# A graph network layer on one core: part of one square moved from ScalarE to the Pool, and x split without its scale factor

## What is computed

```
# first layer: 4 gaussian kernels k over the entries of adj
w[k]  = exp(-0.5 * (adj - mean[k])**2 / (1e-14 + precision[k]**2))
w     = w / sum_k w
ws[k] = sum over the row of w[k]                     # one number per row and kernel
h     = concat_k(ws[k] * (x @ W0[k].T))
x     = layernorm(x + h)
# second layer: one expert per batch, chosen by the batch's mean of x
z     = adj @ x ;  o = z @ expert_w[top1]
y     = relu(batchnorm over all batches of one expert (o))
out   = layernorm(x + y)
```

## Time and profile before

| | |
|---|---|
| timed runs | median 892.62 us, 890.96 to 893.26 |
| the profiled execution | 888.44 us, its span 886.7 us |
| TensorE's mean granted clock | 0.952 |
| PE / DVE / ACT / POOL busy | 751.8 / 754.0 / 766.9 / 687.5 us |
| DMA | 191.71 MB, mean 216 GB/s |

### The profile page before, as it was taken

The page is one execution under the profiler, slowest core; times in us unless marked ns, Lnnn a source line. Parts: engine busy times, 40 slices in busy tenths (PEclk is TensorE's granted clock), DMA queues, the critical chain, the costliest instruction groups (busy, mean ns, idle before and its releaser), DMA issues.

```text
span 886.7 us, 12501 instructions
## 1 busy us (share of the span) xinstructions
PE 751.8 (85%) x3922; PEld 349.1 (39%) x3922; DVE 754.0 (85%) x1639; ACT 766.9 (86%) x774; POOL 687.5 (78%) x773
## 2 busy tenths in 40 slices
PE   1444469899999999999999999999999989996671
PEld 1111124344444444444444444444444434444440
DVE  1999988899999999999999999999999981226994
ACT  5999998999999999999999999999999941116983
POOL 6699999999988888888888888888888441004794
PEclk9966679999999999999999999999999999998996
DMA  8799886898897779777977797789786636219999
GB/s 229 200 282 257 189 243 166 221 202 206 201 240 192 192 190 240 196 194 190 237 198 191 195 240 196 192 189 242 198 190 161 124 141 263 95 64 396 356 383 366
DMA packets 263925, 191.71 MB, mean 216 GB/s; under 512 B 210098, under 2 KB 210098, under 8 KB 262322
## 3 DMA queue, kind: packets, MB, share of 16 engines
q1 hardware_dynamic: 263714, 190.90, 79.3%
q10 hardware_dynamic: 144, 0.00, 0.0%
HBM read 91.78 MB, written 48.76 MB: 159 GB/s over the span
## 4 chain that ended last, share of the span: by engine, by line
ACT 38%; DVE 27%; POOL 19%; PE 9%; issue 4%; DMA 1%; SPq 0%; POOLq 0%; DVEq 0%; ACTq 0%
DVE ps_t L953 19%; ACT wgt L647 13%; ACT ps_t L656 6%; ACT ps_t L658 6%; ACT adj_in L641 5%; ACT ps_t L652 5%; PE ps_z L1118 5%; POOL adj_cut L505 3%; DVE x_in L937 3%; DVE wgt L915 3%; PE ps_o L1136 2%; POOL adj_in L500 2%; POOL x_turn L516 2%; PE ps_t L1136 2%; POOL adj_cut L503 2%
## 5 line engine op out<-in xcount | busy, mean ns | idle before, releaser
L1118 PE MATMUL ps_z<-adjT,x1p 128*128 128x512 f16 x1536 | 341.7, 379 | 0.5 <-POOL x1p L542 0.5
L953 DVE TENSOR_TENSOR ps_t<-ps_t,wgt 128x1024 f32<-128x1024 f32 x192 | 234.8, 1223 | 28.0 <-ACT ps_t L652 26.9
L1104 PE MATMUL ps_h<-w0T,x_turn 128*128 128x512 f16 x768 | 194.5, 407 | 75.1 <-DVE x_in L937 64.2
L915 DVE SCALAR_TENSOR_TENSOR wgt<-wgt,ps_t 128x1024 f32<-128x1024 f32 x192 | 224.7, 1214 | 15.8 <-ACT ps_t L658 15.8
L1118 PEld LDWEIGHTS ps_z<-adjT,x1p 128*128 128x128 f16 x1536 | 150.0, 98 | 181.3 <-POOL x1p L542 1.0
L641 ACT ACTIVATE wgt<-adj_in,neg_mu 128x1024 f32<-128x1024 f32 x192 | 205.6, 1134 | 8.4 <-POOL adj_in L500 8.2
L647 ACT ACTIVATE wgt<-wgt 128x3072 f32<-128x3072 f32 x64 | 176.5, 2758 | 0.0
L1136 PE MATMUL ps_o<-zT,w_sel 128*128 128x512 f16 x696 | 159.7, 379 | 4.8 <-DVE zT L884 3.5
L1104 PEld LDWEIGHTS ps_h<-w0T,x_turn 128*128 128x128 f16 x768 | 75.0, 103 | 184.4 <-issue 105.1
L505 POOL TENSOR_TENSOR adj_cut<-adj_in,adj_cut 128x1024 f16<-128x1024 f32 x64 | 136.6, 2134 | 5.4
L1136 PEld LDWEIGHTS ps_o<-zT,w_sel 128*128 128x128 f16 x696 | 67.9, 98 | 87.7 <-DVE zT L884 4.5
(11 more groups left out here) (220 smaller groups left out, 774.2 us busy)
## 6 DMA issues: line engine op xcount, KB each, us to landing
adj_in<-in_adj_dram SPq DMA_DIRECT2D x64, 512.0 KB, 4.1
x_in<-in_x_dram SPq DMA_DIRECT2D x64, 256.0 KB, 4.3
x_spill<-x_in SPq DMA_DIRECT2D x28, 512.0 KB, 3.4
out_spill<-o_stage SPq DMA_DIRECT2D x50, 256.0 KB, 3.1
w_sel<-w_planes SPq DMA_DIRECT2D x8, 1024.0 KB, 7.5
adjT<-x_spill SPq DMA_DIRECT2D x6, 1024.0 KB, 10.1
out_dram<-adjT SPq DMA_DIRECT2D x5, 1024.0 KB, 6.7
adjT<-out_spill SPq DMA_DIRECT2D x4, 1024.0 KB, 12.7
```

The lines of the kernel that those rows point to most:

```text
L915: v.scalar_tensor_tensor(out=wgt[:, m % 2, j, :], in0=wgt[:, m % 2, j, :], scalar=SUM_SCALE / W0_SCALE, in1=tot, op0=ALU.mult, op1=ALU.mul ...
L953: v.tensor_tensor(tot, tot, wgt[:, n % 2, j, :], ALU.add).then_inc(dve_tot, 1)
L1104: last = te.matmul(ps_h[:, n % 2, :], xT[:, n % 2, left, c, :], w0T[:, right, c, :], start=(c + i == 0), stop=(c == C - 1 and i == 2))
L1118: last = te.matmul(ps_z[:, u % 2, :], x1p[:, b % 2, left, t, k * P:(k + 1) * P], adjT[:, b % 2, right, t, half * HALF:(half + 1) * HALF], ...
```

## The change

The Pool makes the fourth kernel's square for columns 0 to 255 of adj's tile, in place: a `tensor_scalar` with the spread and the shift of the kernel as per-partition scalars, and a `tensor_tensor` product of the result with itself. It does so in iteration n for tile n, behind cut_x(n+2) and ahead of norm_pair, after ScalarE's three other squares of that tile. ScalarE's fourth square covers the other 768 columns, and its fourth exp, which covers all 1024, waits for the Pool's product. The product of x by 16 on the Pool is gone: x is cut as it is, and the constant in L523 is adapted.

```diff
-X_SCALE = 2.0 ** 4
+POOL_SQ = 256
...
                 pool.wait_ge(x_landed[m % X_RING], 16 * (m // X_RING + 1))
-                g.tensor_scalar(tile, tile, X_SCALE, 1.0, ALU.mult, ALU.mult).then_inc(pool_xs, 1)
-                pool.wait_ge(pool_xs, m + 1)
                 wait(pool, x_turned[m % 2], 16 * (m // 2))
...
+            def square(m):
+
+                cols = adj_in[:, m % ADJ_RING, 0:POOL_SQ]
+                pool.wait_ge(act_sq, NK * m + NK - 1)
+                g.tensor_scalar(cols, cols, spread_of[:, SOLO:SOLO + 1], neg_mu[:, SOLO:SOLO + 1],
+                                ALU.mult, ALU.add).then_inc(pool_line, 1)
+                pool.wait_ge(pool_line, m + 1)
+                g.tensor_tensor(cols, cols, cols, ALU.mult).then_inc(pool_sq, 1)
...
-                g.tensor_scalar(rstd[:, p % 2, :], y_mv[:, p % 2, :, 1], X1_SCALE ** -2, LN_EPS * (X_SCALE / X1_SCALE) ** 2,
+                g.tensor_scalar(rstd[:, p % 2, :], y_mv[:, p % 2, :, 1], X1_SCALE ** -2, LN_EPS / X1_SCALE ** 2,
...
                     cut_x(n + 2)
+                if n < TILES:
+                    square(n)
...
-            def square(n, k, to):
-                s.activation(to, adj_in[:, n % ADJ_RING, :], ACT.Square, bias=neg_mu[:, k:k + 1],
+            def square(n, k, to, first=0):
+                s.activation(to, adj_in[:, n % ADJ_RING, first:NR], ACT.Square, bias=neg_mu[:, k:k + 1],
                              scale=spread[k]).then_inc(act_sq, 1)
...
                 act.wait_ge(act_sq, NK * n + NK)
+                act.wait_ge(pool_sq, n + 1)
...
-                    square(n, SOLO, adj_in[:, n % ADJ_RING, :])
+                    square(n, SOLO, adj_in[:, n % ADJ_RING, POOL_SQ:NR], POOL_SQ)
```

More of the change, by code:

```diff
@@ L162, in gnn_program @@
         pool_as, pool_ah, pool_al = (sem(f"pool_{k}") for k in ("as", "ah", "al"))
-        pool_xs, pool_xh, pool_xl = (sem(f"pool_{k}") for k in ("xs", "xh", "xl"))
+        pool_xh, pool_xl = (sem(f"pool_{k}") for k in ("xh", "xl"))
+        pool_line, pool_sq = sem("pool_line"), sem("pool_sq")
         pool_neg, pool_x1, pool_1h, pool_1l = (sem(f"pool_{k}") for k in ("neg", "x1", "1h", "1l"))
```

## The result

The changed kernel takes 901.92 us (median, 901.12 to 905.01), the kernel before 891.79 beside it: a ratio of 1.0133, 95% interval 1.0115 to 1.0151. So it is slower, as forecast, by 10 to 12 us and not by 27.8. The profiled execution took 902.38 us, its span 900.6, against 888.44 and 886.7 before.

A forecast was written before the change was run, and what follows sets the result against it. The four-exp loop through ScalarE and VectorE bounded, then the Pool would: P(60) = 47.3 + 29 x 22.38 + 5.3 = 701.6, tile 63's fourth exp +27.8 us. On 892.6 that gives 920.4 us, range 909 to 931.

The forecast's parts named there:

- The start: Tile 0's fourth exp waits for the Pool's product, moving from 17.76 to 25.2 us: +7.4 us, passed on to later tiles.
- Where the Pool's lateness bites: At even tiles the fourth exp can't start before P(n) + 7.85 us; P(n) is Pool iteration n's start.
- the net cost on the Pool: Per tile on the Pool: square added at 1.40 us, product of x removed at 0.70, net +0.70 us.
- The Pool becomes the bound: In the middle the Pool needs 22.38 us for two tiles, over the kernel's 21.91: 11.19 us a tile.
- ScalarE's loop would take 10.76: ScalarE's chain of exps and fourth square: 256 columns fewer save 0.20 us a tile, from 10.96.
- rival C: Square so cheap that ScalarE's loop bounds again: 12.4 us gained, 7.4 lost at the start; 887.6 us; chance 0.04.
- A: Pool's product of two f32 tensors goes by bytes, 0.84 us; two tiles 22.72 us, +10 us: 930; chance 0.14.
- B: Late start is taken up: P(2) stays at 39.86 us, adj tile 3 getting out another way; 913; chance 0.11.
- D: No change: a Pool square of 0.87 to 0.96 us, two effects cancel; 893 us; chance 0.04 together with between.
- The base: Profiled 888.4 + 27.8 gives 916.2 us; the timed median of 892.6, 4.2 above the profile, makes it 920.4.

The follow-up runs named there:

- Experiment 2: Changed kernel with tile 0 squared by ScalarE alone, its exp waiting for nothing of the Pool; 897.54 us, ratio 1.0066 to the kernel before.
- experiment 9: Changed kernel with 128 columns on the Pool, its product taken with a constant f32 tile instead of with itself; 901.10 us.
- experiment 3: Changed kernel without the Pool's square, ScalarE's whole again; only the product of x by 16 is removed; 891.19 us, ratio 1.0003 to the kernel before.
- experiment 5: Changed kernel with 512 columns of the square on the Pool; 940.86 us.
- experiment 4: Changed kernel with the Pool's product of x by 16 put back; 952.40 us.
- experiment 1: Changed kernel with the Pool's square only from tile 12 on, earlier tiles squared by ScalarE alone; 886.63 us, ratio 0.9959 to the kernel before.
- experiment 8: Changed kernel without the Pool's square, ScalarE squaring only 768 or 256 columns, the others left out; 884.22 and 883.89 us.
- experiment 6: Changed kernel with 128 columns instead of 256 on the Pool; 900.64 us, ratio 1.0122 to the kernel before.

## Why the prediction was wrong

The direction and the start were right, the middle was mis-sized. The direction came out right for part of the reason only: of the forecast 27.8 us, 7.4 belonged to the start and the rest was to build up over all tiles, but in the trace the lag is 17.4 us at tile 10 and shrinks from there. Step by step:

- *The start.* Forecast: fourth exp of tile 0 at 25.2, the Pool on tile 3 at 47.3. Measured: 24.63 and 46.97. Experiment 2 shows that the one hangs on the other.
- *Where the Pool's lateness bites.* Right in kind: at even tiles, by the product's end, 7.5 us into the Pool's iteration (7.85 forecast), and P(60) = P(2) + 29 pairs + the instructions slowed by VectorE. With the measured 21.84 this gives 46.97 + 633.4 + 5.5 = 685.9; the trace has 686.73.
- *The term that failed* is the net cost on the Pool, forecast +0.70 us a tile, measured (21.83 - 20.99) / 2 = +0.42. The product took 0.61 us instead of 0.67 (experiment 9: one tile read twice is cheaper than two). I gave each of the two new instructions a gap, and the first has none: 0.09. And with L511 another gap of 0.12 went away (experiment 3). Together 0.27; times 58 that is 15.7 us, most of the 18.5 us by which I missed (4.5 of these are the base, see the last point).
- *The Pool becomes the bound:* false, but narrowly. It is the bound up to tile 10; after that its 21.84 us are level with the loop's 21.81 to 21.90, and the lead of 0.6 to 1.0 us lasts to the end. With 0.64 and 0.81 us a tile more it bounds the whole middle (experiments 5 and 4), and at 21.89 us a pair the last 16 tiles (experiment 1).
- *ScalarE's loop would take 10.76.* False: 10.88, and in two tiles of each batch 11.01 and 10.95, for a reason that I had not looked for. The row sums end close ahead of the fourth exp even in the trace of before (the third L915 and the L652 after it):

```profile
405.19 1.22 DVE L915 SCALAR_TENSOR_TENSOR wgt<-wgt,ps_t 128x1024 f32<-128x1024 f32 x1
```

```profile
406.61 1.03 ACT L652 ACTIVATE ps_t<-adj_in 128x1024 f32<-128x1024 f32 x1
```

406.41 and 406.61, of which the hand-over takes 0.1: 0.1 us is all that ScalarE could gain. Here the error hardly counts for the time, since it enters three times at the end, but rival C's gain of 12.4 us never was there; with this part of the square free the medians give 6 to 7 and the trace 3.5 at tile 63 (experiment 8).
- *Rivals.* A went the wrong way for this kernel: one tile read twice is cheaper than the row. Two different f32 tiles are dearer than the row, 457 ns against 429 at 128 columns, though less than A's slope would make it (0.18 + 128 x 2.54 ns = 0.51 us). By the Trainium skill (GPSIMD Engine Reference, section 3.1) the read port takes two operands in turn; my estimate from its figure was 0.72 us for this product. The trace has 0.61 for one tile twice, so the measurement goes against the figure here. For two different tiles an estimate from experiment 9, with the fixed part of 186 ns kept and (457 - 186) / 128 = 2.12 ns a column, gives 0.73 for 256 columns, near the page's. B fell with experiment 2's start. C and D needed a square of at most 0.96 us with its gaps, 0.26 over the removal; it costs 0.42 over it.
- *The base.* The profiled execution of before lay 3.4 us under its median and that of after 0.5 over it, so the 13.9 us between the profiles are 10 to 12 between the runs. Adding a profile's difference to a median carries that error.

## What to carry to other kernels

Work that moves to an engine which runs ahead of its consumer costs nothing only where the lead exists: look at the lead at the start too, where it isn't built up yet, and begin the moved part when it is there (here: one condition, from 1.013 to 0.996). Before a step of a loop is shortened, look for what else ends just ahead of the same instruction: a second wait that is met 0.1 us early caps the gain at 0.1 us. When a change moves all later tiles in time, a one-time wait elsewhere can come or go with it (here 1.1 to 1.4 us ahead of tile 14); take it out before traces are compared. When two rates come out within a few per cent of each other, a gap of 0.08 us counts like a duration; take it from a pair of neighbours of the same kind, or keep both results.

## What the runs showed of the hardware

- A Pool product of one f32 tile with itself in place: 399, 612 and 1040 ns at 128, 256 and 512 columns, 1.67 ns a column, against 1.90 for f32 with f16, and 457 ns at 128 columns for two different f32 tiles (experiments 6, 5, 9 and the changed kernel).
- With the product of x by 16 gone, the Pool's faster pace let it meet VectorE's split of the expert weights (L977, two tiles in SBUF) in another place (x_only):

```profile
69.09 2.13 POOL L508 TENSOR_TENSOR adj_cut<-adj_in,adj_cut 128x1024 f16<-128x1024 f32 x1
69.21 3.09 DVE L977 SCALAR_TENSOR_TENSOR zT<-adjT,zT 128x1024 f16<-128x1024 f32 x1
71.18 1.60 POOL L515 TENSOR_SCALAR x_turn<-x_in 128x512 f16<-128x512 f32 x1
```

L977 takes 1.19 us at its best. Begun 0.1 us after L508 it takes 3.09, and L515, begun before L977 ended, 1.60 instead of 0.62. The next fourth exp waited 1.55 us. In the kernel before it was the Pool that was held longest. The Trainium skill (SBUF — State Buffer, section Who interferes with whom) states that a VectorE instruction with two SBUF inputs and a Pool instruction that reads SBUF block each other, the later one until the first is done. These rows agree: L508 ends at 71.22, L977 1.1 us later at 72.30, and L515 0.5 us after that at 72.78.
